# Layer norms applied on GpSimd, a reordered opening, and weighted sums three key tiles behind the scores

## The reference, cut to what matters

```python
x = x + attn(_layernorm(x))                      # 2 heads of 64, rotary positions, causal
x = x + xattn(_layernorm(x), ctx, ctx)           # 16 heads of 8, 1601 keys
x = x + ffn(_layernorm(x))                       # 512 hidden, gelu, a token-dependent part in both weights

def _layernorm(x, eps=1e-05):
    m = jnp.mean(x, axis=-1, keepdims=True)
    v = jnp.var(x, axis=-1, keepdims=True)
    return (x - m) / jnp.sqrt(v + eps)
```

## Time and profile before

| | |
|---|---|
| median of 3 runs | 447.05 us (446.14 to 458.3) |
| the profiled execution | 447.47 us, its span 445.7 us |
| PE, DVE, ACT, POOL busy | 85%, 72%, 67%, 27% of the span |
| first score product (L966) | at 73.2 us |
| last unit's sums copied (L828) | at 427.3 us |

### The profile page before, as it was taken

How to read it: one execution, slowest core, us unless ns; L and a number is a source line. 1 busy time by engine, 2 the same in 40 slices (tenths; PEclk the granted TensorE clock), 3 DMA queues, 4 the chain that set the end, 5 groups by cost and what they waited for, 6 DMA issues and landing times.

```text
span 445.7 us, 9617 instructions
## 1 busy us (share of the span) xinstructions
PE 378.0 (85%) x3640; PEld 175.5 (39%) x3640; DVE 322.0 (72%) x706; ACT 298.6 (67%) x624; POOL 120.4 (27%) x189
## 2 busy tenths in 40 slices
PE   0723798998999998997999998989998999989956
PEld 0421443343344443432444544433544443443325
DVE  2533478969689988877789778898897789874022
ACT  1411013886588878854779878767889888979932
POOL 4541100258300012554700012675300003300010
PEclk9965655999699999967899999998999999999988
DMA  7062236003511712043306033044120231000000
GB/s 259 7 221 80 91 126 219 2 1 112 174 39 54 182 37 88 1 159 112 97 7 157 27 95 91 2 159 163 50 85 25 77 110 50 1 13 3 1 1 12
DMA packets 22316, 35.57 MB, mean 80 GB/s; under 512 B 1622, under 2 KB 19814, under 8 KB 22270
## 3 DMA queue, kind: packets, MB, share of 16 engines
q1 hardware_dynamic: 22270, 34.95, 24.5%
HBM read 19.15 MB, written 11.96 MB: 70 GB/s over the span
## 4 chain that ended last, share of the span: by engine, by line
PE 58%; DVE 21%; ACT 10%; issue 5%; POOL 2%; DMA 2%; SPq 1%; POOLq 0%; ACTq 0%; DVEq 0%
PE wsum L952 19%; DVE part_max L648 12%; PE score L966 12%; PE ring L983 8%; ACT probs L823 5%; PE ring L1077 4%; PE ring L1070 2%; DVE xn L742 2%; PE ring L1119 2%; PE ring L1019 2%; DVE xn L765 2%; PE ring L1110 2%; PE ring L1008 1%; ACT q_unit L834 1%; PE ring L1002 1%
## 5 line engine op out<-in xcount | busy, mean ns | idle before, releaser
L648 DVE TENSOR_REDUCE part_max<-ring 128x1 f32<-128x401 f32 x512 | 260.5, 567 | 52.9 <-PE ring L983 52.3
L823 ACT ACTIVATE probs<-score 128x512 f32<-128x512 f32 (+1 forms) x416 | 223.0, 597 | 56.0 <-PE score L966 53.2
L983 PE MATMUL ring<-k_unit,q_unit 51*128 51x401 bf16 x512 | 148.6, 362 | 10.9 <-DVE part_max L648 7.3
L952 PE MATMUL wsum<-probs,v_unit 128*32 128x256 f32 (+1 forms) x1664 | 139.5, 406 | 2.7 <-ACT unit_ctx L828 2.1
L966 PE MATMUL score<-q_unit,k_unit 51*128 51x256 bf16 (+1 forms) x832 | 127.9, 284 | 9.0 <-ACT probs L823 6.6
L966 PEld LDWEIGHTS score<-q_unit,k_unit 51*128 51x128 bf16 (+1 forms) x832 | 47.5, 98 | 106.2 <-ACT probs L823 60.4
L983 PEld LDWEIGHTS ring<-k_unit,q_unit 51*128 51x128 bf16 x512 | 48.6, 97 | 32.9 <-DVE part_max L648 21.3
L952 PEld LDWEIGHTS wsum<-probs,v_unit 128*32 128x32 f32 (+1 forms) x1664 | 34.8, 110 | 52.9 <-issue 27.4
L526 POOL TENSOR_TENSOR max_parts<-neg_max,c_sb 128x8 bf16<-128x8 f32 x16 | 3.3, 209 | 150.3 <-DVE neg_max L652 150.3
L878 ACT ACTIVATE v_aug<-ring 128x128 f32<-128x128 f32 x48 | 9.4, 283 | 25.3 <-PE ring L1077 25.3
L1008 PE MATMUL ring<-c_sb,xn 128*128 128x128 f32 x24 | 6.2, 350 | 20.8 <-DVE xn L674 12.8
(11 more groups left out here) (106 smaller groups left out, 323.4 us busy)
## 6 DMA issues: line engine op xcount, KB each, us to landing
k_unit<-k_rows SPq DMA_DIRECT2D x32, 300.2 KB
v_unit<-v_aug SPq DMA_DIRECT2D x16, 234.0 KB, 5.8
ctx_sb<-ctx_t SPq DMA_DIRECT2D x4, 800.5 KB, 7.3
k_rows<-k_parts SPq DMA_DIRECT2D x4, 601.5 KB, 3.5
k_rows<-k_parts SPq DMA_DIRECT2D x4, 599.2 KB, 3.7
k_rows<-k_parts SPq DMA_DIRECT2D x4, 401.0 KB, 4.1
k_rows<-k_parts SPq DMA_DIRECT2D x4, 399.5 KB, 4.3
q_unit<-q_rows SPq DMA_DIRECT2D x32, 48.0 KB
```

What stands on the lines that cost most here:

```text
L648: v_.tensor_reduce(part_max[:, par, q, head, hp, c:c + 1], ring[s][:, 0:CW], AX.X, ALU.max)\
L823: a_.activation(probs[0:rows, i % PB, :], score[i % EB][0:rows, :], ACT.Exp)\
L952: last = mm(wsum[32 * j:32 * j + 32, 0:S], v_unit[0:rows, u, VQ * t + VW * j:VQ * t + VW * j + 32], probs[0:rows, i % PB, S * (j // 2):S * ...
L983: mm(ring[s][:, 0:CW], q_unit[rows, u, hp, P * q:P * (q + 1)], k_unit[rows, u, L * hp + (CW - 1) * c:L * hp + (CW - 1) * c + CW], start=Tr ...
```

## The change

- **Norms.** In the loop `ln1` (sequences 1 to 3), `ln2` (1 to 3) and `ln3` (0 to 2) are applied by POOL, for `ln2` and `ln3` directly after it has taken the power. For sequence 0, and for the last `ln3`, they stay on DVE. `ln3` has no place of its own in the table any more.
- **Opening.** The statistics of sequence 0 come first, its power is taken apart from the others'. `prob_norm` of sequence 0 goes from POOL to DVE, ahead of the split of K3; `xT`, `qk`, `qks` of sequence 1 go to earlier places. The queries of unit 0 no longer pass through DRAM: six products with a 0/1 table `pick` place them in a ring bank, and ACT copies them to the query tile. The table adds 384 columns to the transfer of the tables. Values are made two key tiles at a time (`U0` to `U6`), after each four M.
- **Lag.** `PV(v, t-3)` in place of `PV(v, t-2)`; `norm`, `OT` and `Wo` one tile later.

```diff
-    for i in range(4):
-        plan += [("M", 0, k) for k in range(8 * i, 8 * i + 8)] + [("prep", f"V{i}", 0)]
-    plan += [("prep", "load", 0), ("ctx", 1)] + [("M", 1, k) for k in range(4)] + [("mT", 0)]
+    for i in range(7):
+        plan += [("M", 0, k) for k in range(4 * i, 4 * i + 4)] + [("prep", f"U{i}", 0)]
+    plan += [("M", 0, k) for k in range(28, MU)] + [("prep", "load", 0), ("ctx", 1)]
...
-        if t == 3 and v:
+        if t == 4 and v:
             plan.append(("norm", v - 1))
...
-        if t >= 2:
-            plan.append(("PV", v, t - 2))
+        if t >= 3:
+            plan.append(("PV", v, t - 3))
...
-    (0, 6): [("prep", "pn", 1), ("post", "OT", -1)], (0, 8): [("post", "Wo", -1)],
-    (0, 12): [("prep", "av", 1), ("post", "ln3", -1)],
+    (0, 6): [("prep", "pn", 1)], (0, 7): [("post", "OT", -1)], (0, 9): [("post", "Wo", -1), ("prep", "K0", 1)], (0, 10): [("prep", "pT0", 1), ("prep", "pT1", 1)], (0, 11): [("prep", "K1", 1)],
+    (0, 12): [("prep", "av", 1)],
-    (1, 4): [("prep", "ln2", 1), ("prep", "store0", 1)], (1, 6): [("prep", "x2T", 1)],
+    (1, 4): [("prep", "store0", 1)], (1, 6): [("prep", "x2T", 1)],
...
                         g.tensor_tensor(rstd2[:, :], var2[:, :], C("pow")[:, 0:QT], ALU.pow).then_inc(rstd2_set, 1)
+                        if b:
+                            pool.wait_ge(rstd2_set, b + 1)
+                            for q in range(QT):
+                                last = g.tensor_scalar(xn2[:, q, :], x1[:, q, :], mv2[:, q, 0:1], rstd2[:, q:q + 1],
+                                                       ALU.subtract, ALU.mult)
+                            last.then_inc(xn2_done, 1)
...
+                    if nb == 0:
+                        dve.wait_ge(prsum_done, 1)
+                        for q in range(QT):
+                            cols = slice(0, P) if q == 0 else slice(P, 3 * P)
+                            for h in range(HA):
+                                last = v_.tensor_scalar(prob_norm[:, h, cols], prob_self[:, h, cols],
+                                                        prob_rsum[:, q, h:h + 1], None, ALU.mult)
+                        last.then_inc(norm_done, 1)
...
+                elif name == "pick":
+                    s, n = take(item)
+                    a_.activation(q_unit[:, 0, :, :].rearrange("p h n -> p (h n)"), ring[s][:, :], ACT.Copy)\
+                        .then_inc(drained[s], 1)
...
-                    pe.wait_ge(unit_in[u], 96 * (v // UB + 1))
+                    pe.wait_ge(unit_in[u], 96 * (v // UB + 1) - (64 if u == 0 else 0))
+                    if v == 0:
+                        s, n = RING["prep", "pick", 0]
+                        pe.wait_ge(drained[s], n + 1)
...
+                elif name == "pick":
+                    pe.wait_ge(q_split, 4)
+                    pe.wait_ge(tables_in, 16)
                     s = take(item)
+                    pick = C("pick").bitcast(BF16).rearrange("p (h t r) -> p h t r", h=2, t=3)
+                    for hp in range(2):
+                        for part in range(3):
+                            last = mm(ring[s][:, S * hp:S * (hp + 1)], pick[:, hp, part, :], q_parts[:, part, :],
+                                      start=part == 0, stop=part == 2)
+                    last.then_inc(filled[s], 1)
```

More of the change, by code:

```diff
@@ L107, in constants @@
     put("blocks", np.eye(4, dtype=np.float32))
+    pick = np.zeros((P, 2, 3, P), np.uint16)
+    for hp in range(2):
+        for par in range(2):
+            for t, part in enumerate(Q_PART):
+                for d in range(DX):
+                    pick[2 * DX * par + 2 * d + hp, hp, part, HALF * par + MR + DX * t + d] = 0x3F80
+    put("pick", pick.view(np.float32))
     put("ones", np.full((MR, L), TWO_ONES, np.float32))
@@ L142 @@
 }
-PREP_FIRST = ["ln1", "xT", "qk", "qks", "K0", "K1", "e0", "e1", "K2", "K3", "store0", "soft", "pn", "v", "pT0", "pT1",
-              "av", "store1", "wo", "ln2", "x2T", "q", "split"]
-PREP_SECOND = ["ln1", "xT", "qk", "qks"]
+FIRST = [("ln1", 0), ("ln1", 1), ("xT", 0), ("qk", 0), ("qks", 0), ("K0", 0), ("K1", 0), ("e0", 0), ("e1", 0), ("soft", 0),
+         ("pn", 0), ("K2", 0), ("K3", 0), ("store0", 0), ("v", 0), ("xT", 1), ("qk", 1), ("pT0", 0), ("pT1", 0), ("av", 0),
+         ("store1", 0), ("wo", 0), ("ln2", 0), ("x2T", 0), ("q", 0), ("split", 0), ("qks", 1), ("pick", 0)]
 POST_LAST = ["OT", "Wo", "ln3", "x3T", "low0", "low1", "h0", "h1", "out"]
@@ L225, with last_values, value_tiles @@
 RING = ring_slots()
+def last_values(b):
+    return ("prep", "V3" if b else "U6", b)
+def value_tiles(name):
+    width = 4 if name[0] == "V" else 2
+    t0 = width * int(name[1])
+    return t0, min(width, KT_FULL - t0), t0 + width > KT_FULL
 def score_index(v, t, n):
@@ L546, in _ @@
                     name, b = item[1:]
-                    if name == "K1" or name == "K3" and b:
+                    if name == "ln1" and b:
+                        s, n = RING["prep", "xT", b - 1]
+                        pool.wait_ge(filled[s], n + 1)
+                        pool.wait_ge(rstd1_set, 2)
+                        for q in range(QT):
+                            last = g.tensor_scalar(xn1[:, q, :], x_all[:, b, q, :], mv1[:, b, q, 0:1],
+                                                   rstd1[:, b, q:q + 1], ALU.subtract, ALU.mult)
+                        last.then_inc(xn1_done, 1)
+                    elif name == "K1" or name == "K3" and b:
                         h = int(name[1]) // 2
@@ L580, in _ @@
                             .then_inc(q_split, 1)
-                    elif name == "pn":
+                    elif name == "pn" and b:
                         pool.wait_ge(prsum_done, b + 1)
@@ L600, in _ @@
                     g.tensor_tensor(rstd3[:, :], var3[:, :], C("pow")[:, 0:QT], ALU.pow).then_inc(rstd3_set, 1)
+                    if b < B - 1:
+                        pool.wait_ge(rstd3_set, b + 1)
+                        for q in range(QT):
+                            last = g.tensor_scalar(xn3[:, q, :], x2[:, q, :], mv3[:, q, 0:1], rstd3[:, q:q + 1],
+                                                   ALU.subtract, ALU.mult)
+                        last.then_inc(xn3_done, 1)
                     g.tensor_tensor(x2_b2[:, :, :], x2[:, :, :],
@@ L670, in prep @@
                 name, nb = item[1:]
-                if name == "ln1":
+                if name == "ln1" and nb == 0:
                     dve.wait_ge(rstd1_set, 1)
@@ L873, in prep @@
                                 act.wait_ge(values_in[u], 16 * nb)
-                    t0 = 4 * int(name[1])
-                    tn = min(4, KT_FULL - t0)
+                    t0, tn, short = value_tiles(name)
                     s, n = take(item)
```

64 lines of the change are left out of this document (35 added, 29 removed), and 1 row of the table SIDE.

## The result

| | before | changed |
|---|---|---|
| median | 449.89 us (4 runs) | 415.17 us (4 runs, 411.83 to 417.18) |
| ratio | | 0.9246, 95% interval 0.9122 to 0.9371 |
| profiled execution | 447.47 us | 417.18 us, span 415.4 us |
| first score product | 73.2 us | 60.8 us |
| first M product | 50.2 us | 38.9 us |

A forecast was written before the change was run, and what follows sets the result against it. No single engine was named as bound: DVE norms blocked beside POOL splits, PE idling and low clock cost the loop, a serial chain the opening. 12.2 + 19.3 + 1.2 = 32.7 off 447.5 gives 415 us; eight in ten, 405 to 432.

The forecast's parts named there:

- the likeliest case: Case A, whole kernel: opening, second units and loop ln1 all gain as summed, 415 us, own range 406 to 421; chance 0.48.
- First norm, probabilities, queries: Opening: norm 2.0 us earlier, turn of the probabilities 5.3 earlier including that, first M 11.0 earlier at 39.2.
- The keys: Opening, unit 0: keys stored from about 25.87 us, leaving 13 us for store and load before the first M.
- The M of unit 0: Opening: half-long value portions leave DVE gaps, 1.2 us counted as gained; PE nearly the bound at low clock.
- Second units: Second units of sequences 0 to 2: without DVE's norm pairs the clock stays up, 23.0 us each, 19.3 us gained.
- POOL's norms: Loop norms on POOL: 0.60 us to double for one of 128x128, pairs 1.2 us, covered by POOL's idle time.
- The two `ln1`: Two loop ln1 on DVE, 0.59 us each among back-to-back maxima: moving them gains 1.2 us.
- The lag: Loop, PV three tiles behind the scores: removes no wait of PE, counted as 0.
- Rival B: Clock still falls in second units; only about 10 us of maxima waits and 12.2 in the opening saved: 425; chance 0.22.
- C: PE or ACT takes over at once, or POOL's queue delays the turn; only 13.4 us gained: 434; chance 0.10.
- D: The opening doesn't shorten: 6 us less there, 421 with the full loop, 427 with a half; chance 0.10.

The follow-up runs named there:

- a_halves: The changed kernel with the keys of unit 0 loaded in two halves, the first once its stores landed: 412.2 us, ratio 0.9202.
- b_spread: The changed kernel with keys of unit 0 in two halves and values of sequence 0 made in PE's waits of the opening: 411.2 us, ratio 0.9246.
- n_norms: The kernel before with only the norms of the loop moved to GpSimd: 436.2 us, ratio 0.9710.
- n_clear: The kernel before with the loop's norms left on DVE but listed where POOL splits no keys: 429.8 us, ratio 0.9567.
- n_lag: The kernel before with only PV three tiles behind the scores and norm, OT and Wo one tile later: 451.4 us, ratio 1.0095.
- a_pv2: The changed kernel with PV back at two tiles, norm, OT and Wo left one tile later: 417.2 us, ratio 0.9331.
- a_lag2: The changed kernel with PV back at two tiles and norm, OT and Wo taken back too: 423.6 us, ratio 0.9455.
- b_clear: The kernel before with the new opening, the loop's norms on DVE clear of POOL's key splits, and the old lag: 417.8 us, ratio 0.9375.

## Why the prediction was right

The time was 415 us, as forecast; the likeliest case was the one that came. The agreement to 0.2 us is luck: the profiled execution is 30.3 us shorter than that of before by their spans, where the sum has 32.7, and the medians lie 34.7 apart. Its steps fared less evenly.

- **First norm, probabilities, queries**: right. First transposed product at 7.79 us (8.0 said), turn of the probabilities at 23.30 (23.8), first M at 38.91 (39.2), first score at 60.8 (61.0). The four prob_norm were done at 22.74 us, not 23.4: one of them did end only with POOL's split (22.33), but it was the third and not the first, and only one was left behind it. By the prediction's own figures its case would end at 23.9; the turn didn't hang on it, for PE came to it at 23.3. The six `pick` products took 0.82 us at full clock, where 0.5 was reckoned by columns from four M products in 0.52 us; those overlap (one lasts 0.36 by its record), and the 1.0 that was taken covers it.
- **The keys**: wrong in its reason. I gave them 13 us and called them covered. They were the last to come: the queries were on their place at 37.0, the keys 1.9 us later. The start came out right only because the sum had the queries there 2.2 us too late: 0.5 at the turn, 1.3 in the chain from it to the last query part (12.2 us, not 13.5) and 0.4 in `pick`. a_halves shows the wait and takes it away.
- **The M of unit 0**: 21.9 us where 21.8 followed from the sum; PE was busy 19.82 us of it at the low clock, and b_spread, which takes value products out of it, is shorter. This fits PE's work as the bound, as suspected; the ring banks that the values hold went with them, and the two aren't told apart.
- **Second units**: the mechanism held (n_norms, n_clear), the term was too small. I took 23.0 us for each; they took 22.2, 21.6 and 21.6, so 22.9 us came from them in place of 19.3. The 3.5 us of PE work that the last sequence lacks cost nothing extra.
- **POOL's norms**: 0.79 us for one of 128x128, inside the bounds of 0.60 to double; 1.58 for a pair against 0.59 on a free DVE, 2.7 times and not the twice that the prediction's 1.2 stands for.
- **The two `ln1`**: 0.4 us from unit 3, 0.2 from unit 7, in place of 1.2.
- **The lag**: here a step failed, though its sentence on PV was right. "I count 0" was said of the whole edit, and taking all of it back costs 8 us, part of them by how long the clock then stays low. With the places one tile later units 4, 8 and 12 are also 0.8, 0.8 and 0.3 us shorter than before, which no term had; n_lag shows the same. PV's own tile is worth nothing (a_pv2), but `Wo` one tile later puts POOL's norm behind the maxima's parts. I had seen this ("so a turn is never kept by it") and had not priced what it would cost otherwise, a PE wait of 2.5 us and a fall of the clock. The edit is part of moving the norms, not an edit by itself: alone it made the kernel 1% slower, and the norms alone brought 13 of the 20 us expected of them.
- **What came in unforeseen**: unit 11, 4.4 us longer by the fall behind the gelu's table, unit 10 1.3 us and unit 0 1.3 us longer. The first of these differs between executions, as above. They offset the terms that I had too small, and the sum was right partly because of this.

Rival B (the clock falls in the second units all the same) and C are gone by the stages above, and D by the first score product at 60.8. The short wait at 189.40 that spoke for B stood behind a pair too, that of `ln3` (L765, 185.76 to 188.86), and went with it. B's warning holds for other places: units 0, 11 and 14.

## What to carry to other kernels

When one engine's elementwise instruction takes several times its free length, look at what GpSimd does in the same microseconds: moving the instruction by one or two tiles in the list was worth at least as much as moving it to another engine (19 against 13 us). Work that is moved to an engine with idle time has to be placed behind what others wait for on it; otherwise a short queue there becomes a wait of the tensor engine, and behind the wait came 3 to 14 us of slower clock. Edits that look separate in a diff should be priced with each other's state: the sum of the three alone was 24 us, of the three together 34.

## What the runs showed of the hardware

- The clock's fall behind a wait of PE has a price of its own, and it isn't the same each time. In a_lag2 a wait of 2.48 us was followed by 13.7 us at the 1.2 GHz level, and that unit was 5.1 us longer; in n_norms a wait of 2.47 us at the same place was followed by 3.4 us of it, and that unit was 1.1 us longer than before. In the changed kernel two stretches with PE busy 1.28 and 1.48 of 2 us were followed by 10.2 us of it. Behind a wait of 1.22 us the clock fell in n_clear and stayed up in before, a_lag2 and b_clear.
- How long the low level lasts after the opening differs between executions. In the profiles here unit 0 took 21.6 to 22.8 us where the clock was back 6 to 12 us after the first score, 24.6 to 25.0 us where it took 15 to 17, and 26.8 or 26.9 us where it stayed low for about 21. Before (6.0 us, unit 0 21.6) and n_norms (20.7 us, unit 0 26.9) have the same program up to there. This alone is 5 us, about as much as several of the edits, and so may be a good part of the intervals above. What decides it wasn't found.
- The clock also stood low with PE at work all the time: from 73.5 to 94 us n_norms shows PE busy 20.23 of 20.50 us at 0.50.
- A subtract-and-multiply of 128x128 float32 took 0.34 us by its record on a free DVE, 0.79 on GpSimd, and up to 1.87 on DVE beside a GpSimd split (106.69 us in the kernel before).
